# One block of a transformer with routed experts: the order of the opening's work is changed

## The chip, the cores and the metric

The kernel runs on one core of a Trainium2 chip. The metric is the device time of one execution in microseconds; before the change it is 890.94 us, the median of three runs (890.64 to 897.05).

## The reference

Input `x` is 32 batches of 256 tokens of 128 features. Each batch has its own modulation, made from a 32 x 128 condition `c`. An attention of 16 heads of 8 features stands ahead of a layer of 32 experts of which each token uses two. Cut to what matters:

```python
mod = (silu(c) @ wmod).reshape(32, 6, 1, -1)
sa, ca, ga, sb, cb, gb = (mod[:, i] for i in range(6))
ga = (2 * (ga >= 0) - 1) * maximum(abs(ga), 0.25)          # gb too
h = layernorm(x) * (1 + ca) + sa
Q, gate = split(h @ Wq + bq); K = h @ Wk + bk; V = h @ Wv + bv
Q, K = rmsnorm(Q, qn_w), rmsnorm(K, kn_w)                  # per head, 8 features
attn = softmax(Q @ K.T / sqrt(8))
x = x + ga * ((attn @ V * sigmoid(gate)) @ Wo + bo)
h = layernorm(x) * (1 + cb) + sb
vals, idx = top_k(softmax(h @ router_w.T), 2)
x = x + gb * sum_over_chosen(vals * (h @ expert_weights[idx]))
```

## The kernel before, in words

The kernel is written engine by engine. Each engine runs its own list of instructions in order and waits on semaphores; `sem` makes one, `then_inc` raises it, `wait` or `wait_ge` waits for it. Transfers raise a semaphore by 16 when they have landed.

After an opening, `run` goes through steps `s`. In a step each engine works on ten batches at different stages: `ahead` is batch s + 1, `b0` is batch s, `b1` the one before it, and so on. A batch goes through layer norm and projection (`b0`), splitting of q and k into bf16 parts which are stored to DRAM (`b1`) and loaded again as heads (`q_aug`, `k_aug`), row maxima of the scores (`b2`), exponentials and products with v (`b3`), output projection (`b4`), second norm and routing (`b5` to `b8`). Routed rows are scattered to DRAM (`xs_d`), and groups of them are multiplied by their expert's weights (`we`). The last steps drain this pipeline.

What the change touches is the opening and the first three steps:

- The condition. ScalarE takes an exponential into `sc` (L901), VectorE makes the silu from it by three operations (`sgn` L1181, `mag` L1183, `sc` L1185), TensorE transposes it and multiplies it by the first columns of `wmod` (L1706, L1710), ScalarE copies these as `saT` and `caT` (L956, L957).
- The bias. TensorE multiplies `saT` by the projection weights `wqkv` (L1714) once all eight pieces of weights and biases have landed (`w_ld`). VectorE adds the plain biases (`bias`, L1245), SyncE stores the sum to DRAM (L499) and loads it back, broadcast over partitions, as `bias_p` (L503). VectorE needs `bias_p` for `qkvg` (L1279), the projection's output. Ahead of the bias add, VectorE clears `zeros` (L1242).
- GpSimd scales the projection weights by `caT` (`scale_wqkv`, L679), and clears `k_aug`, `q_aug` (L659, L660) and `v_aug` (L684), of which it then sets one column of each head to one (L687).
- Five small late loads, issued by ScalarE (L961, L963): `rw` (router weights), `wo`, `bo_b` (output weights and bias), and the two norm weights into `w_col`. They share the semaphore `loads`. VectorE scales `w_col` (L1284) behind `qkvg`, and uses `bo_b` at the end of `mod_rows_out` (L1269), in step 1. TensorE transposes `rw` (L1758), ScalarE copies the result as `rwT` (L965).
- `squares` of batch 0 (L951) on ScalarE, whose sums VectorE takes (L1290) for the norms of q and k.
- In the step in which batch 0 is `b2`, `gate_exp` issues on ScalarE the store of the modulation `mod_d` (L976), the load of the expert weights `we` (L977, 2 MB in pieces of 512 bytes) and a store of zeros to the lead rows of four experts (`zero_leads`, L914, 256 KB). In the same step SyncE issues the four stores of batch 1's parts (`store_parts`, L530 and L533) and waits for them (`parts_st`) before it loads batch 1's heads (`load_heads`, L550, L554), on which TensorE's scores (L1779) wait.

Of the kernel before, what the change touches and what calls it, by code (L numbers as in the profile page):

```python
# [38 lines left out]
H, HD = 16, 8  # L39
# [142 lines left out]
def build(nc, x, Wq, bq, Wk, bk, Wv, bv, Wo, bo, qn_w, kn_w, router_w, expert_w, c_in, wmod, out):  # L182
# [10 lines left out]
    def sem(name):  # L193
        return ctx.enter_context(nc.semaphore(name))
# [4 lines left out]
    with ctx:  # L199
# [149 lines left out]
        loads, w_ld = sem("loads"), sem("w_ld")  # L349
        c_ld, wm_ld = sem("c_ld"), sem("wm_ld")  # L350
# [56 lines left out]
        def wait(eng, s, n):  # L407

            if isinstance(n, int) and n <= 0:
                return  # L410
            eng.wait_ge(s, n)
# [229 lines left out]
        def _(gp):  # L641
# [17 lines left out]
            nc.gpsimd.memset(k_aug[0][:].bitcast(F32), 0.0).then_inc(gp_const, 1)  # L659
            nc.gpsimd.memset(q_aug[0][:].bitcast(F32), 0.0).then_inc(gp_const, 1)  # L660
# [21 lines left out]
            scale_wqkv(Batch(0, 0, 0))  # L682
            for i in range(2):
                nc.gpsimd.memset(v_aug[i][:], 0.0).then_inc(gp_const, 1)  # L684
# [213 lines left out]
        def _(act):  # L898
# [60 lines left out]
            h1_transposed(Batch(0, 0, 0))  # L959
            for dst, src in ((rw[:], router_w), (wo[:], Wo), (bo_b[:], bo.partition_broadcast(NB))):  # L960
                act.dma_start(dst, src).then_inc(loads, 16)  # L961
            for k, w in enumerate((qn_w, kn_w)):
                act.dma_start(w_col[:, k:k + 1], w.unsqueeze(1).unsqueeze(2).broadcast_to([HD, H, 1])).then_inc(loads, 16)  # L963
            act.wait_ge(rwT_ps, 1)
            nc.scalar.activation(rwT[:], mx_ps[0][:].rearrange("p a b -> p (a b)")[:, 0:E], ACT.Copy).then_inc(rwT_done, 1)  # L965
            act.wait_ge(dve_const, 4)

            @of_batch
            def gate_exp(b):
# [4 lines left out]
                if b.n == 0:  # L974
                    act.wait_ge(mod_sb, 2)
                    act.dma_start(mod_d, mod[:]).then_inc(mod_st, 16)  # L976
                    act.dma_start(we[:].rearrange("k (e n) -> k e n", e=E), expert_w.rearrange("e k n -> k e n")).then_inc(we_ld, 16)  # L977
                if b.n < 8 * SETS:
                    zero_leads(b.n // 8, 4 * (b.n % 8), 4)

            @of_batch
            def high_part(b):

                wait(act, qkT_ps, b.n + 1)
# [102 lines left out]
            def attention_step(s, ahead, b0, b1, b2, b3, b4, b5, b6, b7, b8):  # L1087
# [35 lines left out]
                norms_seed(ahead, b0, b4)  # L1123
                router_exp(b7)
# [49 lines left out]
        def _(dve):  # L1174
# [72 lines left out]
            def mod_rows_out():  # L1247
# [20 lines left out]
                dve.wait_ge(loads, 16 * 5)  # L1268
# [14 lines left out]
            dve.wait_ge(loads, 16 * 5)  # L1283
# [418 lines left out]
        def _(pe):  # L1702
# [54 lines left out]
            pe.wait_ge(loads, 16 * 5)  # L1757
# [290 lines left out]
```

## Time and profile before

| | |
|---|---|
| median of three timed runs | 890.94 us (890.64 to 897.05) |
| the profiled execution | 899.71 us |
| its span, first to last instruction | 897.9 us |
| instructions | 23227 |
| mean granted clock of TensorE | 0.923 |

The span is what the rows below are measured in; the time of the same execution has 1.8 us around it. Times in the rows are microseconds from the start of the span. A row with an engine's name and a q (SPq, ACTq) is the issue of a transfer by that engine's queue, not the transfer; DMA rows tell of the transfers.

### The profile page before, as it was taken

The page shows a single profiled execution, that of the slowest core. Times are in us where ns is not written, and L with a number is a line of the kernel's source. Part 1 is how long each engine was busy: PE and PEld are TensorE (multiplying, and loading weights), DVE is VectorE, ACT ScalarE, POOL GpSimd, SP SyncE. Part 2 cuts the span into 40 slices and gives each one's busy share as a digit, 9 for nine tenths or more (in the row PEclk, how much of TensorE's full clock was granted, in tenths as well). Part 3 has the DMA queues.
Part 4 walks back from the last instruction along what each step waited for, and adds up shares of the span by engine and source line. Part 5 has one row for each costly group of instructions (what it writes and reads, how often), then busy time and mean ns, then how long its engine had stood idle before and what let it go on. Part 6 is the DMA issues. An engine that isn't in the chain of part 4 may idle for free. (4 is left out here: it accounts for less than half of the span.)

```text
span 897.9 us, 23227 instructions
## 1 busy us (share of the span) xinstructions
PE 697.3 (78%) x6142; PEld 467.0 (52%) x6142; DVE 666.9 (74%) x2007; ACT 576.5 (64%) x1313; POOL 528.4 (59%) x864
## 2 busy tenths in 40 slices
PE   3458898998899999898998798888988897564500
PEld 1225555655556666566665465556665556454400
DVE  5658888999998888887878877787877866643333
ACT  2227787888778887778887676677865775324400
POOL 4213346666566665555677666656666666575665
PEclk9559999999999999999999999999998999879955
DMA  2374556645656777666677666666666545789932
GB/s 72 78 187 107 149 134 155 165 129 160 143 154 170 183 186 182 168 170 176 178 199 210 169 167 173 159 167 167 175 160 160 156 143 168 205 232 271 287 97 78
DMA packets 189553, 147.98 MB, mean 165 GB/s; under 512 B 20596, under 2 KB 173908, under 8 KB 189428
## 3 DMA queue, kind: packets, MB, share of 16 engines
q1 hardware_dynamic: 122516, 99.41, 43.2%
q10 hardware_dynamic: 58720, 30.30, 11.9%
q0 software_dynamic: 8192, 16.79, 6.8%
q8 instruction: 56, 0.92, 0.5%
q14 instruction: 69, 0.57, 0.2%
HBM read 84.91 MB, written 60.95 MB: 162 GB/s over the span
## 5 line engine op out<-in xcount | busy, mean ns | idle before, releaser
L1310 DVE TENSOR_REDUCE negmax<-mx_ps 128x2 f32<-128x512 f32 x512 | 339.7, 685 | 64.2 <-PE mx_ps L1779 62.8
L1006 ACT ACTIVATE pr<-st_ps 128x512 f32<-128x512 f32 x512 | 289.8, 596 | 75.1 <-PE st_ps L1814 72.1
L1779 PE MATMUL mx_ps<-k_aug,q_aug 126*128 126x256 bf16 x1024 | 201.7, 282 | 66.2 <-DVE negmax L1310 36.9
L1814 PE MATMUL st_ps<-q_aug,k_aug 128*128 128x256 bf16 x1024 | 179.4, 277 | 11.7 <-ACT xsT L1042 8.4
L818 POOL DMA_INDIRECT xs_d<-h,slot x128 | 129.5, 1012 | 72.3 <-DVE slot L1413 48.9
L1779 PEld LDWEIGHTS mx_ps<-k_aug,q_aug 126*128 126x128 bf16 x1024 | 80.3, 99 | 160.5 <-issue 153.4
L833 POOL DMA_INDIRECT yg<-ys_d,gidx x128 | 124.8, 975 | 52.0 <-issue 36.7
L1828 PE MATMUL o_ps<-pr,v_aug 128*32 128x256 f32 x2048 | 137.0, 385 | 0.8 <-ACT oT L1012 0.2
L1814 PEld LDWEIGHTS st_ps<-q_aug,k_aug 128*128 128x128 bf16 x1024 | 98.6, 102 | 45.3 <-issue 30.2
L695 POOL TENSOR_TENSOR qn<-qkvg,rstd 128x256 f32<-128x256 f32 x64 | 39.2, 636 | 72.8 <-DVE rstd L1226 72.2
L1828 PEld LDWEIGHTS o_ps<-pr,v_aug 128*32 128x32 f32 x2048 | 54.8, 109 | 49.5 <-issue 28.4
L1492 DVE TENSOR_SCALAR yw<-yg,p_all 128x128 f32<-128x128 f32 x64 | 16.1, 297 | 69.0 <-DMA yg<-ys_d,gidx 44.8
L1042 ACT ACTIVATE xsT<-st_ps 128x512 f32<-128x512 f32 x72 | 42.6, 592 | 28.6 <-PE st_ps L1906 21.0
L1752 PE MATMUL misc<-wq_b,hT 128*128 128x400 f32 x128 | 58.1, 542 | 3.4 <-ACT hT L945 3.4
L1279 DVE TENSOR_TENSOR qkvg<-misc,bias_p 128x400 f32<-128x400 f32 x64 | 36.7, 575 | 28.8 <-PE misc L1752 22.3
L1012 ACT ACTIVATE oT<-o_ps 128x256 f32<-128x256 f32 x128 | 48.4, 378 | 9.6 <-PE o_ps L1828 9.5
L736 POOL TENSOR_TENSOR xga<-x_o,mod_o 128x256 f32<-128x256 f32 x31 | 22.5, 727 | 49.6 <-DMA mod_o<-mod_d 49.4
L1906 PE MATMUL st_ps<-ident,xs_sb 128*128 128x128 f32 x288 | 46.2, 285 | 6.1 <-DMA xs_sb<-xs_d 6.1
L1920 PE MATMUL st_ps<-we,xsT 128*128 x328 | 46.1, 284 | 5.9 <-issue 3.5
L708 POOL TENSOR_TENSOR parts<-rest,parts 128x512 bf16<-128x512 f32 x32 | 37.0, 1157 | 21.0 <-ACT parts L994 20.9
L1920 PEld LDWEIGHTS st_ps<-we,xsT 128*128 128x128 f32 x328 | 40.6, 194 | 12.2 <-issue 12.2
L1837 PE MATMUL misc<-ident,oT 128*128 128x128 f32 x256 | 41.3, 287 | 1.4 <-DVE table L1458 0.7
(169 smaller groups left out, 1192.5 us busy)
## 6 DMA issues: line engine op xcount, KB each, us to landing
ys_d<-ys_sb ACTq DMA_DIRECT2D x72, 256.0 KB
xs_sb<-xs_d SPq DMA_DIRECT2D x246, 64.0 KB
q_aug<-q_d SPq DMA_DIRECT2D x64, 192.0 KB
mod_o<-mod_d SPq DMA_DIRECT2D x32, 256.0 KB
bias_p<-bias_d SPq DMA_DIRECT2D x32, 200.0 KB, 4.6
q_d<-parts SPq DMA_DIRECT2D x32, 192.0 KB, 2.3
k_d<-parts SPq DMA_DIRECT2D x32, 192.0 KB, 2.5
k_aug<-k_d SPq DMA_DIRECT2D x64, 96.0 KB
```

The lines of the kernel that those rows point to most:

```text
L818: nc.gpsimd.indirect_dma_start(xs_d[chunk.set], bass.IndirectOffsetOnAxis(ap=slot[:, b.par, k:k + 1], axis=0), h2[:, b.par, k % TB, :], No ...
L833: nc.gpsimd.indirect_dma_start(yg[:, n % FB, k, :], None, ys_d[chunk.c], bass.IndirectOffsetOnAxis(ap=gidx[:, pair:pair + 1], axis=0)).the ...
L1006: nc.scalar.activation(pr[:, h % PR], st_ps[score_bank(b, h)][:], ACT.Exp, scale=SCALE).then_inc(exp_d, 1)
L1012: nc.scalar.activation(oT[:, g, :], o_ps[:, 0:NT], ACT.Copy).then_inc(oT_d, 1)
L1042: nc.scalar.activation(xsT[g % XB][:], in_bank(g), ACT.Copy).then_inc(xsT_d, 1)
L1310: v.tensor_reduce(negmax[:, :, h], mx_ps[h % 2][:], AX.X, ALU.max, negate=True).then_inc(mx_d, 1)
L1752: t_.matmul(bank[:, 0:QKVG], hT[:, t * P:(t + 1) * P], wq_b[:, b.par], start=True, stop=True).then_inc(qkv_ps, 1)
L1779: last = t_.matmul(mx_ps[h % 2][:, qc], q_aug[b.par][0:MROW, h, qc * P:(qc + 1) * P], k_aug[b.par][0:MROW, h, :], start=True, stop=True)
L1814: last = t_.matmul(st_ps[score_bank(b, h)][:, kc], k_aug[b.par][:, h, kc * P:(kc + 1) * P], q_aug[b.par][:, h, :], start=True, stop=True)
L1828: last = t_.matmul(o_ps[32 * j:32 * j + VW, 0:NT], v_aug[b.par][:, kc, h, :], pr[:, h % PR, kc, :], start=(kc == 0), stop=(kc == TB - 1))
L1906: last = t_.transpose(in_bank(g)[:, k * P:(k + 1) * P], xs_sb[:, g % XB, k, :], ident[:])
L1920: last = t_.matmul(out_bank(g)[:, k * P:(k + 1) * P], xsT[g % XB][:, k * P:(k + 1) * P], we[:, bass.ds(columns[k], P)], start=True, stop=True)
```

## The change

Three groups of work are put in another order; no operation is added or removed.

```diff
+        wc_ld = sem("wc_ld")
...
-            nc.gpsimd.memset(k_aug[0][:].bitcast(F32), 0.0).then_inc(gp_const, 1)
-            nc.gpsimd.memset(q_aug[0][:].bitcast(F32), 0.0).then_inc(gp_const, 1)
...
             scale_wqkv(Batch(0, 0, 0))
+            nc.gpsimd.memset(k_aug[0][:].bitcast(F32), 0.0).then_inc(gp_const, 1)
+            nc.gpsimd.memset(q_aug[0][:].bitcast(F32), 0.0).then_inc(gp_const, 1)
             for i in range(2):
                 nc.gpsimd.memset(v_aug[i][:], 0.0).then_inc(gp_const, 1)
...
+            for k, w in enumerate((qn_w, kn_w)):
+                act.dma_start(w_col[:, k:k + 1], w.unsqueeze(1).unsqueeze(2).broadcast_to([HD, H, 1])).then_inc(wc_ld, 16)
             for dst, src in ((rw[:], router_w), (wo[:], Wo), (bo_b[:], bo.partition_broadcast(NB))):
                 act.dma_start(dst, src).then_inc(loads, 16)
-            for k, w in enumerate((qn_w, kn_w)):
-                act.dma_start(w_col[:, k:k + 1], w.unsqueeze(1).unsqueeze(2).broadcast_to([HD, H, 1])).then_inc(loads, 16)
-            act.wait_ge(rwT_ps, 1)
-            nc.scalar.activation(rwT[:], mx_ps[0][:].rearrange("p a b -> p (a b)")[:, 0:E], ACT.Copy).then_inc(rwT_done, 1)
-            act.wait_ge(dve_const, 4)
...
                     act.dma_start(mod_d, mod[:]).then_inc(mod_st, 16)
-                    act.dma_start(we[:].rearrange("k (e n) -> k e n", e=E), expert_w.rearrange("e k n -> k e n")).then_inc(we_ld, 16)
                 if b.n < 8 * SETS:
                     zero_leads(b.n // 8, 4 * (b.n % 8), 4)
+                if b.n == 0:
+                    act.dma_start(we[:].rearrange("k (e n) -> k e n", e=E), expert_w.rearrange("e k n -> k e n")).then_inc(we_ld, 16)
...
             def high_part(b):
 
+                if b.n == 0:
+                    act.wait_ge(dve_const, 4)
...
                 norms_seed(ahead, b0, b4)
+                if s == 0:
+                    act.wait_ge(rwT_ps, 1)
+                    nc.scalar.activation(rwT[:], mx_ps[0][:].rearrange("p a b -> p (a b)")[:, 0:E], ACT.Copy).then_inc(rwT_done, 1)
...
-                dve.wait_ge(loads, 16 * 5)
+                dve.wait_ge(loads, 16 * 3)
                 v.tensor_tensor(mod[:, GABO * P:SB * P], mod[:, GA * P:GABO * P], bo_b[0:NB, :], ALU.mult).then_inc(mod_sb, 1)
...
-            dve.wait_ge(loads, 16 * 5)
+            dve.wait_ge(wc_ld, 32)
             v.tensor_scalar(w_col[:], w_col[:], W_SCALE, None, ALU.mult).then_inc(dve_const, 1)
...
-            pe.wait_ge(loads, 16 * 5)
+            pe.wait_ge(loads, 16 * 3)
             t_.transpose(mx_ps[0][:].rearrange("p a b -> p (a b)")[:, 0:E], rw[:], ident[0:E, 0:E]).then_inc(rwT_ps, 1)
```

What stands in a row on the engines is as follows. On GpSimd, in the opening, before:

```order
L657 IOTA past_pad 128x1
L659 MEMSET k_aug 128x2048
L660 MEMSET q_aug 128x2048
L679 TENSOR_TENSOR wq_b<-wqkv,caT 128x400
L684 MEMSET v_aug 128x1024 x2
L687 MEMSET v_aug 128x32 x2
L695 TENSOR_TENSOR qn<-qkvg,rstd 128x2x16x8 x2
```

And now on GpSimd, at the same place (line numbers are one or more off for the lines added and moved):

```order
L658 IOTA past_pad 128x1
L678 TENSOR_TENSOR wq_b<-wqkv,caT 128x400
L682 MEMSET k_aug 128x2048
L683 MEMSET q_aug 128x2048
L685 MEMSET v_aug 128x1024 x2
L688 MEMSET v_aug 128x32 x2
L696 TENSOR_TENSOR qn<-qkvg,rstd 128x2x16x8 x2
```

The two largest memsets have moved from ahead of the scaling to behind it. On ScalarE, from batch 0's transposed rows `hT` to the parts of its q and k, before:

```order
L945 ACTIVATE hT<-misc 128x256
L961 DMA rw<-in_L_ffn_router_w 32x128
L961 DMA wo<-in_L_attn_Wo 128x128
L961 DMA bo_b<-in_L_attn_bo 32x128
L963 DMA w_col<-in_L_attn_qn_w 128x1x1
L963 DMA w_col<-in_L_attn_kn_w 128x1x1
L965 ACTIVATE rwT<-mx_ps 128x32
L951 ACTIVATE sq<-qkvg 128x512
L928 ACTIVATE lnv<-mv,eps 128x66
L933 ACTIVATE y<-lnv 128x66
L987 ACTIVATE parts<-misc,w_col 128x256 x2
```

And now on ScalarE, at the same place:

```order
L946 ACTIVATE hT<-misc 128x256
L962 DMA w_col<-in_L_attn_qn_w 128x1x1
L962 DMA w_col<-in_L_attn_kn_w 128x1x1
L964 DMA rw<-in_L_ffn_router_w 32x128
L964 DMA wo<-in_L_attn_Wo 128x128
L964 DMA bo_b<-in_L_attn_bo 32x128
L952 ACTIVATE sq<-qkvg 128x512
L929 ACTIVATE lnv<-mv,eps 128x66
L934 ACTIVATE y<-lnv 128x66
L1127 ACTIVATE rwT<-mx_ps 128x32
L988 ACTIVATE parts<-misc,w_col 128x256 x2
```

The norm weights are now the first two of the five loads, and `rwT` has moved behind the norms' logarithm and exponential. On ScalarE, in the step in which batch 0 is `b2`, before:

```order
L973 ACTIVATE eg<-qkvg 128x32
L976 DMA mod_d<-mod 32x640
L977 DMA we<-in_L_ffn_expert_weights 128x32x128
L914 DMA xs_d<-zeros 128x4x128
L945 ACTIVATE hT<-misc 128x256
```

And now on ScalarE, at the same place:

```order
L971 ACTIVATE eg<-qkvg 128x32
L974 DMA mod_d<-mod 32x640
L915 DMA xs_d<-zeros 128x4x128
L978 DMA we<-in_L_ffn_expert_weights 128x32x128
L946 ACTIVATE hT<-misc 128x256
```

The expert weights and the zero leads have changed places.

## Rows read from the trace of the kernel before

**Rows 1.** The page, busy us (share of the span) of each engine

```profile
PE 697.3 (78%) x6142; PEld 467.0 (52%) x6142; DVE 666.9 (74%) x2007; ACT 576.5 (64%) x1313; POOL 528.4 (59%) x864
```

**Rows 2.** Window for L1006: us, ACT busy (count), PEclk, DMA share, GB/s

```profile
78.40:96.70 18.30, 8.79 (x16) 1.00 0.50 131
```

**Rows 3.** Timeline of VectorE: start, us, line, operation, [idle before <-releaser]

```profile
3.05 3.60 DVE L1181 TENSOR_SCALAR sgn<-sc 32x128 f32<-32x128 f32 x1
...
10.26 0.91 DVE L1242 MEMSET zeros<- 128x1024 f32 x1 [0.16 <-issue]
11.71 0.56 DVE L1245 TENSOR_TENSOR bias<-st_ps,bqkv 32x400 f32<-32x400 f32 x1 [0.54 <-PE st_ps L1714]
17.11 1.06 DVE L1279 TENSOR_TENSOR qkvg<-misc,bias_p 128x400 f32<-128x400 f32 x2 [4.83 <-DMA bias_p<-bias_d]
18.56 0.17 DVE L1284 TENSOR_SCALAR w_col<-w_col 128x2 f32<-128x2 f32 x1 [0.39 <-DMA w_col<-in_L_attn_kn_w]
...
19.61 0.69 DVE L1290 TENSOR_REDUCE mv<-sq 128x64 f32<-128x512 f32 x1
```

**Rows 4.** Instructions on tile sgn: duration ns min/median/max, first and last start

```profile
L1260 DVE TENSOR_SCALAR sgn<-mod x2: 208/211/214, 27.0 to 29.5; 32x128 f32<-32x128 f32 x2
```

**Rows 5.** Timeline of GpSimd

```profile
3.04 1.79 POOL L659 MEMSET k_aug<- 128x2048 f32 x1
...
4.78 1.79 POOL L660 MEMSET q_aug<- 128x2048 f32 x1
...
10.18 0.85 POOL L679 TENSOR_TENSOR wq_b<-wqkv,caT 128x400 f32<-128x400 f32 x1 [3.61 <-ACT caT L957]
...
10.97 1.84 POOL L684 MEMSET v_aug<- 128x1024 f32 x2
...
22.02 1.22 POOL L695 TENSOR_TENSOR qn<-qkvg,rstd 128x256 f32<-128x256 f32 x2 [8.94 <-DVE rstd L1226]
```

**Rows 6.** Timeline of TensorE, the bias matmul

```profile
10.09 1.51 PE L1714 MATMUL st_ps<-wqkv,saT 128*32 128x400 f32 x2 [0.38 <-ACT saT L956]
```

**Rows 7.** Timeline of ScalarE, opening

```profile
3.98 0.44 ACTq L906 DMA_DIRECT2D bqkv<-in_L_attn_bq  x1
...
14.94 0.62 ACTq L963 DMA_DIRECT2D w_col<-in_L_attn_kn_w  x1
...
18.95 0.62 ACT L951 ACTIVATE sq<-qkvg 128x512 f32<-128x512 f32 x1
```

**Rows 8.** Timeline of ScalarE, issues of expert weights and zero leads

```profile
45.06 0.83 ACTq L977 DMA_DIRECT2D we<-in_L_ffn_expert_weights  x1
...
45.92 5.68 ACTq L914 DMA_DIRECT2D xs_d<-zeros  x1
...
71.41 0.44 ACTq L914 DMA_DIRECT2D xs_d<-zeros  x1
```

**Rows 9.** Timeline of SyncE, stores of batch 1's parts

```profile
46.37 1.48 SPq L530 DMA_DIRECT2D q_d<-parts  x3
47.89 0.50 SPq L533 DMA_DIRECT2D k_d<-parts  x1
```

**Rows 10.** DMA, 46-51 us, then 51-57.2 us (q10 ScalarE's, q1 SyncE's): packets, MB

```profile
q10 hardware_dynamic: 553, 1.13, 86.3%
...
k_d<-parts SPq DMA_DIRECT2D x1, 192.0 KB, 9.2
...
q10 hardware_dynamic: 1015, 1.23, 60.1%
q1 hardware_dynamic: 1216, 0.59, 33.2%
```

**Rows 11.** Timeline of TensorE, scores of batch 1

```profile
61.77 1.01 PE L1779 MATMUL mx_ps<-k_aug,q_aug 126*128 126x256 bf16 x4 [6.17 <-DMA k_aug<-k_d]
```

**Rows 12.** DMA issues, 3 to 4.5 us: count, KB each, us to landing

```profile
bqkv<-in_L_attn_bq ACTq DMA_DIRECT2D x1, 2.0 KB, 3.3
```

**Rows 13.** DMA issues, 70 to 75 us, stores of batch 2's parts

```profile
k_d<-parts SPq DMA_DIRECT2D x1, 192.0 KB, 2.4
```

## The prediction

> **What bounds the kernel now.** I read the page first, for the shares: TensorE is busy 78% of the span, VectorE 74%, so no engine is saturated as a whole [rows 1]. Over most of the span the work is a pipeline of one batch per step; a step in it takes 18.3 us, in which ScalarE does the sixteen exponentials of a batch [rows 2]. None of its code changes, and nothing in it waits for a fixed moment. What the opening saves should therefore arrive at the end whole, and what it loses too. So I read the first 62 us engine by engine, and look for the last wait of each stage.
>
> Stage A is the conditioning path. VectorE's first real operation, `sgn`, starts at 3.05 us and takes 3.60 us [rows 3]. The same operation on the same tile shape takes 0.21 us later [rows 4]. In that stretch GpSimd runs two memsets of 1.79 us, until 6.57 us; `sgn` ends 0.08 us after the second [rows 3, 5]. The reader is to see an operation that is long only as long as GpSimd writes. From it hang `sc`, the transposes and matmuls on TensorE, `saT`, and with that the bias matmul at 10.09 us [rows 6].
>
> Stage B is the bias round trip: the add at 11.71 us, the store, the broadcast load; VectorE waits 4.83 us for it and starts `qkvg` at 17.11 us [rows 3]. The projection itself was ready earlier, so stage B decides.
>
> Stage C starts when `qkvg` ends at 18.17 us. VectorE waits 0.39 us more for the second norm weight, whose transfer was issued last of five, at 14.94 us; ScalarE does the squares at 18.95 us, behind `rwT`, for which it waits until all five transfers have landed [rows 3, 7].
>
> Stage D is the expert weights. ScalarE issues them at 45.06 us, and then stands 5.68 us in the issue of the zero leads, from 45.92 us on [rows 8]; `hT` and all else of it wait behind. SyncE issues the four stores of batch 1's parts from 46.37 us on; the last, `k_d`, at 47.89 us, lands 9.2 us later, at 57.09 us, and only then can the heads' loads be issued [rows 9, 10]. TensorE waits 6.17 us for these, until 61.77 us [rows 11]. Thus stage D's last wait is the transfer of the parts, not ScalarE.
>
> **The change, part by part.** *GpSimd's memsets behind the scaling.* `sgn` takes 0.21 instead of 3.60 us: minus 3.39 us at `sc`. The whole of it can't be kept, since the bias matmul also waits for all eight pieces of weights and biases. The last is issued by ScalarE at 3.98 us and lands 3.3 us later, at 7.28 us [rows 7, 12]. So the bias matmul starts at about 7.32 instead of 10.09 us: **minus 2.77 us**. Upstream work leaves room for that: shifted by 3.39 us it would stand at 6.70 us, or some tenths later, as batch 0's rows have to land as well. The add, the store, the broadcast load and `qkvg` follow unchanged, so `qkvg` starts at 14.34 us.
>
> The memsets themselves aren't gone: the scaling runs 7.3 to 8.2 us, then `k_aug` and `q_aug` (2 x 1.79 us) and `v_aug` (1.84 us) until some 13.7 us, the ones behind them to about 14 us. I cost them at nothing, as the bias round trip covers them: VectorE next has `qkvg` at 14.34 us, and GpSimd batch 0's normalised q and k, which stood at 22.02 us and move to 18.9 [rows 5]; SyncE's loads into `k_aug` and `q_aug` come later still. Without this cover they would cost up to 5.4 us. Inside the cover VectorE has two operations: the `zeros` memset and the bias add. Before, `zeros` took 0.91 us beside GpSimd's scaling and the add 0.56 us beside the `v_aug` memset, hardly more than `qkvg`'s 0.53 us each for as many columns [rows 3, 5]; I take both as undisturbed.
>
> *Norm weights first, `rwT` and a wait later.* The two norm weights are issued three transfers sooner and land before `qkvg` ends, so VectorE's 0.39 us go. The squares no longer stand behind `rwT`; then VectorE's order decides: `w_col`, statistics, aggregate, and the reduction at 19.61 us, all 0.38 us earlier with `w_col`. **Minus 0.38 us.** The three transfers behind them are issued later by the two issues of the norm weights. The router weights wait for the engine that does nothing before batch 0's q and k are there; the output bias is next read behind these; nobody waits. `rwT` now stands behind the norms' seed, where ScalarE waits for TensorE's transposes of them in any case. The wait on the scaled norm weights is long met where it now stands.
>
> *Zero leads ahead of the expert weights.* This frees ScalarE of most of 5.68 us: a later issue of zero leads takes 0.44 us [rows 8]. `hT` could come some microseconds sooner. But TensorE's next wait is on the parts, so **this part of it is worth nothing** on the path. It is `hT`'s followers on TensorE and VectorE that move into the idle time before 61.77 us. What is late next is `k_d`. In 46 to 51 us all packets are ScalarE's queue, 553 of them, none of SyncE's; in the 6 us after, SyncE's 1216 share with 1015 of ScalarE's [rows 10]. The parts are therefore served once the expert weights' descriptors are out. The new order changes this in two ways. The expert weights are asked for one issue later, 0.44 us, and with them the parts: plus 0.44. The 0.26 MB of zeros no longer move beside the parts; 51 to 57.2 us moved 1.23 + 0.59 MB, 0.29 MB per us [rows 10], so these are 0.9 us; most of it, I take 0.8: minus 0.8. Sum: **minus 0.36 us**, with bounds of plus 0.9 (the zeros' own bytes also push the expert weights back, and the parts gain nothing) and minus 0.9.
>
> One rule speaks on this place. The Trainium skill (DMA: Bandwidth & Descriptors, Queues, rings and completion order) says that each transfer engine takes turns between the queue rows that have work. By that rule the parts would move from 47 us on, with half of the rate, and the order of zeros and expert weights would be indifferent: minus 3.15 instead of minus 3.51. The trace disagrees here, with no packet of SyncE's queue before 51 us [rows 10], so I keep the sum from the rows.
>
> **Sum.** 2.77 + 0.38 + 0.36 = 3.51 us less. The profiled execution has a span of 897.9 us and a time of 899.71; so I expect a span of 894.4. The three timed runs have a median of 890.94, 8.8 us under the profiled time; the opening is the same work in both, and the difference is carried over: 890.94 - 3.5 = **887.4 us**.
>
> **The rivals.** *R1, the opening gives less (0 to 2 us).* Something other than the memsets holds `sgn`, or the weights land later than 7.28 us, or a few microseconds at the start are absorbed by waits further on. For it: only one row shows the long `sgn`. Against it: `sgn` ends with the memset to 0.1 us. Time: about 890.
>
> *R2, the memsets hold VectorE at a worse place.* If batch 0's statistics are late by about 0.8 us, the `zeros` memset reaches VectorE when GpSimd's row of memsets has begun. If it is held as `sgn` was, through one memset after the other, it starts at 13.7 and the bias add, queued behind it, at 14.6 us against 11.71: 2.9 us later than before. With the other parts kept (minus 0.74) that is plus 2.2: 893.1 us. It ends slower than before once the add starts later than 12.45 us. Against it: both operations ran undisturbed beside GpSimd's work, though `zeros` beside the scaling only.
> The Trainium skill (SBUF — State Buffer, SBUF: two separate sides) calls the shared ports an exclusive lock, held for a whole instruction by whoever starts first; that is what would do it. It agrees with the `sgn` row. A memset in place of `zeros` beside a memset is in no row here.
>
> *R3, the parts get ahead of the expert weights.* The expert weights' issue now ends at some 46.3 us in the old trace's times, and the first store of the parts is issued at 46.37. If the engines come to serve the stores first or in turns, `k_d` lands as batch 2's did, 2.4 us after its issue instead of 9.2 [rows 13]: up to 6.8 us, at least 2 to 5 of them real, since other waits (the maxima of batch 0, the norms) come next. Time: 882 to 886, say 884. Against it: three quarters of the stores are issued well behind.
>
> *R4, no change at all can be seen* because the steady part goes another way: timed runs of the same code stand at 890.64, 890.94 and 897.05. A median that falls on such an upper run would be near 893.
>
> **How the numbers follow.** My forecast (a gain of 2.0 to 4.7 us) 0.60; R1 0.17; R2 0.06; R3 0.10; R4 0.07. The likeliest case's own range is 886 to 889. For 8 in 10 the range takes in R1, most of R3 and the lower part of R2 and R4: 883.5 to 893. One per cent is 8.9 us, about what a measurement of this kernel can tell from no change; only R3 with everything on top reaches it (0.03), and only R4 with more bad luck on the other side (0.02). So 0.95 stays within 1%.
>
> **What would show it.** Right: `sgn` near 0.2 us with GpSimd idle beside it; the bias matmul at 7.2 to 7.5 us; `zeros` 0.9 and the bias add near 0.56 us; `qkvg` at 14.1 to 14.6; the squares directly behind it; the issue of the zero leads under 1 us; SyncE's first packets of the parts still some 5 us after their issue; TensorE's first scores of batch 1 at about 58.3 us; steps of 18.3 us thereafter. Wrong: `sgn` still long; the bias add after 12 us; `k_d` landing in under 4 us; or the step starts ahead by 3.5 us at 100 us and not at the end, which would mean the steady part absorbs a head start.

## The result and the profile after

The changed kernel takes 889.82 us, the median of 20 runs (885.75 to 897.29); the kernel before takes 893.96 us beside it, also 20 runs (889.85 to 898.71). The ratio is 0.9952, with a 95% interval of 0.9932 to 0.9973: 4.3 us less, between 2.4 and 6.1. That is less than 1%. The absolute time is 2.4 us above the forecast of 887.4, since the kernel before, measured more often, itself takes 3.0 us more than the 890.94 from which the forecast was counted. The profiled execution of the changed kernel took 894.12 us, with a span of 892.3 against 897.9 us. The busy times of the engines hardly move (TensorE 696.9 us against 697.3 [rows 1]), except VectorE's, which falls from 666.9 to 662.7 us: 3.45 of these 4.2 us are `sgn`, whose waiting the profile counts as busy time. No engine has less work to do; the gain is waiting time.

The timeline of VectorE in the changed kernel, the counterpart of [rows 3]. Columns as there: start, duration, engine, line, operation, and in brackets the idle time ahead of it and what ended it.

```profile
3.05 0.15 DVE L1185 TENSOR_SCALAR sgn<-sc 32x128 f32<-32x128 f32 x1
...
6.85 0.16 DVE L1236 SCALAR_TENSOR_TENSOR shift<-mv,rstd 128x2 f32<-128x2 f32 x1
7.17 0.91 DVE L1246 MEMSET zeros<- 128x1024 f32 x1 [0.16 <-issue]
8.60 0.56 DVE L1249 TENSOR_TENSOR bias<-st_ps,bqkv 32x400 f32<-32x400 f32 x1 [0.52 <-PE st_ps L1718]
...
14.50 1.06 DVE L1283 TENSOR_TENSOR qkvg<-misc,bias_p 128x400 f32<-128x400 f32 x2 [5.33 <-DMA bias_p<-bias_d]
...
15.47 0.16 DVE L1288 TENSOR_SCALAR w_col<-w_col 128x2 f32<-128x2 f32 x1
...
16.41 0.65 DVE L1294 TENSOR_REDUCE mv<-sq 128x64 f32<-128x512 f32 x1
```

`sgn` went from 3.60 to 0.15 us, and everything behind it is about 3 us earlier. One number stands against that: the wait of `qkvg` for the broadcast bias, 5.33 us, was 4.83.

GpSimd in the changed kernel, the counterpart of [rows 5]: the scaling first, the memsets behind it, and batch 0's normalised q and k.

```profile
7.08 0.85 POOL L678 TENSOR_TENSOR wq_b<-wqkv,caT 128x400 f32<-128x400 f32 x1 [3.98 <-DMA bqkv<-in_L_attn_bq]
...
7.87 1.80 POOL L682 MEMSET k_aug<- 128x2048 f32 x1
...
9.61 1.80 POOL L683 MEMSET q_aug<- 128x2048 f32 x1
...
11.36 1.85 POOL L685 MEMSET v_aug<- 128x1024 f32 x2
...
18.80 1.22 POOL L696 TENSOR_TENSOR qn<-qkvg,rstd 128x256 f32<-128x256 f32 x2 [5.32 <-DVE rstd L1230]
```

TensorE, the bias matmul and the first scores of batch 1 (before: [rows 6, 11]):

```profile
6.95 1.54 PE L1718 MATMUL st_ps<-wqkv,saT 128*32 128x400 f32 x2 [0.69 <-DMA bqkv<-in_L_attn_bq]
...
57.94 1.01 PE L1783 MATMUL mx_ps<-k_aug,q_aug 126*128 126x256 bf16 x4 [9.04 <-DMA k_aug<-k_d]
```

The scores start 3.83 us earlier, and TensorE waits for them longer than before, 9.04 against 6.17 us: what used to be spent behind ScalarE's stall is now spent waiting for the parts.

ScalarE around the expert weights (before: [rows 8]), and then SyncE's stores (before: [rows 9]):

```profile
41.60 0.45 ACTq L915 DMA_DIRECT2D xs_d<-zeros  x1
...
42.27 0.83 ACTq L978 DMA_DIRECT2D we<-in_L_ffn_expert_weights  x1
```

```profile
43.12 1.51 SPq L531 DMA_DIRECT2D q_d<-parts  x3
44.68 0.68 SPq L534 DMA_DIRECT2D k_d<-parts  x1
```

The DMA view of the changed kernel for 41 to 46 us and then 46 to 51 us (queue, packets, MB, share; for an issue its KB and us to landing), the counterpart of [rows 10]:

```profile
q10 hardware_dynamic: 768, 0.74, 59.2%
q1 hardware_dynamic: 1, 0.00, 0.0%
...
k_d<-parts SPq DMA_DIRECT2D x1, 192.0 KB, 8.6
...
q10 hardware_dynamic: 713, 1.46, 84.1%
q1 hardware_dynamic: 638, 0.32, 23.2%
```

ScalarE's 5.68 us in the issue of the zero leads are gone, and SyncE's queue still moves next to nothing (one packet) until about 46 us. `k_d` lands 8.6 us after its issue, at 53.28 us. At first it can't be the rate of transfer alone that the parts wait for: from 44 to 45 us, when the expert weights and the first stores of the parts have been asked for, 0.08 MB move, and from 48 to 49 us 0.36 MB. The stall was a symptom of the expert weights; the wait that decides is their other symptom, and it is still there.

### The profile page after: what moved, and what is told of

It reads as the page before. It is cut to its first block and busy times, and to the rows that moved or that the text cites. A ratio compares the mean times of both kernels' runs of the same rounds, so it can differ in the third digit from the quotient of the medians.

```text
span 892.3 us, 23227 instructions
## 1 busy us (share of the span) xinstructions
PE 696.9 (78%) x6142; PEld 467.6 (52%) x6142; DVE 662.7 (74%) x2007; ACT 576.9 (65%) x1313; POOL 530.2 (59%) x864
## 5 line engine op out<-in xcount | busy, mean ns | idle before, releaser
L819 POOL DMA_INDIRECT xs_d<-h,slot x128 | 129.9, 1015 | 70.9 <-DVE slot L1417 47.6
L1756 PE MATMUL misc<-wq_b,hT 128*128 128x400 f32 x128 | 57.2, 535 | 1.2 <-ACT hT L946 1.2
```

Source lines behind the costliest of these rows:

```text
L819: nc.gpsimd.indirect_dma_start(xs_d[chunk.set], bass.IndirectOffsetOnAxis(ap=slot[:, b.par, k:k + 1], axis=0), h2[:, b.par, k % TB, :], No ...
L1756: t_.matmul(bank[:, 0:QKVG], hT[:, t * P:(t + 1) * P], wq_b[:, b.par], start=True, stop=True).then_inc(qkv_ps, 1)
```

## The experiments

Medians and ratios come from several runs of each kernel against the kernel before on the same chip, except for e6, e7 and e8, of which there is one execution each. e5 to e8 were measured at another time than the rest, and beside them the kernel before takes 962.28 us instead of some 893, for a reason that the record doesn't show (it names the same chip for e1 to e4); their times are compared only with that, and their opening, which is the same there to 0.3 us, by the trace.

### e1: GpSimd's memsets alone

The kernel before, with this one edit:

```diff
-            nc.gpsimd.memset(k_aug[0][:].bitcast(F32), 0.0).then_inc(gp_const, 1)
-            nc.gpsimd.memset(q_aug[0][:].bitcast(F32), 0.0).then_inc(gp_const, 1)
     (scaling of the weights for batch 0)
+            nc.gpsimd.memset(k_aug[0][:].bitcast(F32), 0.0).then_inc(gp_const, 1)
+            nc.gpsimd.memset(q_aug[0][:].bitcast(F32), 0.0).then_inc(gp_const, 1)
```

> Only GpSimd's two memsets go behind the scaling; the five late loads, rwT, the expert weights and the zero leads stay as before. My theory: this is the larger part of the gain. sgn about 0.15 us, the bias matmul at about 6.95 us (3.1 us earlier), the four stores of batch 1's parts some 3 us earlier than before, but k_d still 9.2 us from issue to landing, scores of batch 1 at about 58.6 us, ScalarE's issue of the zero leads still near 5.7 us; in all 3 us less. On a question that the changed kernel leaves open: its bias round trip (add to qkvg) took 5.90 us instead of 5.40. If that comes of the norm weights' loads being issued first, here it is 5.40 again and qkvg starts at 14.0; if it comes of something else at the earlier moment, it is 5.9 here too. Rival (the memsets don't hold sgn): sgn stays near 3.6 us and nothing moves.

Measured: 889.44 us (12 runs) against 892.65 (35 runs), ratio 0.9953 (0.9926 to 0.9979). This is the ratio of the whole change. VectorE in e1:

```profile
8.72 0.56 DVE L1245 TENSOR_TENSOR bias<-st_ps,bqkv 32x400 f32<-32x400 f32 x1 [0.69 <-PE st_ps L1714]
...
14.12 1.06 DVE L1279 TENSOR_TENSOR qkvg<-misc,bias_p 128x400 f32<-128x400 f32 x2 [4.84 <-DMA bias_p<-bias_d]
```

From the add to `qkvg` e1 takes 5.40 us, just as before (11.71 to 17.11), and its `qkvg` is 0.38 us ahead of that of the full change. ScalarE's issue of the zero leads still takes 5.57 us, `k_d` lands 8.7 us after its issue, and yet the scores of batch 1 start at 57.74 us, not later than with the full change (58.6 had been expected). So the memsets' move carries all of the gain that can be measured.

### e2: the norm weights first, alone

The changed kernel, with GpSimd's memsets and the expert weights where they were before.

> Only the norm weights go first among the late loads, with a semaphore of their own, and rwT and the wait on the scaled weights go later; memsets, expert weights and zero leads as before. My theory: w_col without a wait behind qkvg, the reduction of batch 0's squares 0.4 us after where it would be counted from qkvg, so that GpSimd's first normalisation is 0.4 us nearer to qkvg (4.5 instead of 4.9 us). If the loads' order costs the bias round trip 0.5 us, qkvg itself is at 17.6 instead of 17.1 us and the sum is nothing; else the sum is minus 0.4 us. Either way the time can't be told from before's.

Measured: 893.41 us (12 runs), ratio 1.0005 (0.9974 to 1.0035). VectorE in e2:

```profile
11.72 0.56 DVE L1249 TENSOR_TENSOR bias<-st_ps,bqkv 32x400 f32<-32x400 f32 x1 [0.54 <-PE st_ps L1718]
...
17.62 1.06 DVE L1283 TENSOR_TENSOR qkvg<-misc,bias_p 128x400 f32<-128x400 f32 x2 [5.34 <-DMA bias_p<-bias_d]
...
18.59 0.16 DVE L1288 TENSOR_SCALAR w_col<-w_col 128x2 f32<-128x2 f32 x1
```

`w_col` no longer waits 0.39 us, as predicted. But `qkvg` starts at 17.62 instead of 17.11, 0.51 us later, with an unchanged add ahead of it. The wait was moved one operation forward, and `w_col` itself stands at 18.59 against 18.56. Batch 0's first `qn` on GpSimd comes at 21.92 against 22.02 us: from `qkvg` to `qn` it saves 0.61 us, the later `qkvg` costs 0.51, and 0.10 us is left.

### e7: the old order of the late loads in the changed kernel

```diff
-            for k, w in enumerate((qn_w, kn_w)):
-                act.dma_start(w_col[:, k:k + 1], ...).then_inc(wc_ld, 16)
     (router weights, output weights, output bias)
+            for k, w in enumerate((qn_w, kn_w)):
+                act.dma_start(w_col[:, k:k + 1], ...).then_inc(wc_ld, 16)
```

> The changed kernel, with the five late loads in the order of before (router weights, output weights and bias, then the norm weights), the norm weights keeping their own semaphore. If the norm weights' loads in front cost the bias round trip, as the two runs with and without them point to, qkvg starts 5.40 us after the bias add again, at 14.0 instead of 14.5 us; w_col then waits about 0.3 us for the second norm weight, the squares don't, and GpSimd's first normalisation comes at 18.6 instead of 18.8 us. If not, all of it stays.

VectorE in e7 (one execution), with GpSimd's scaling in a fence of its own:

```profile
7.10 0.82 DVE L1236 SCALAR_TENSOR_TENSOR shift<-mv,rstd 128x2 f32<-128x2 f32 x1
8.09 0.91 DVE L1246 MEMSET zeros<- 128x1024 f32 x1 [0.16 <-issue]
8.92 0.50 DVE L1249 TENSOR_TENSOR bias<-st_ps,bqkv 32x400 f32<-32x400 f32 x1
...
14.30 1.05 DVE L1283 TENSOR_TENSOR qkvg<-misc,bias_p 128x400 f32<-128x400 f32 x2 [4.88 <-DMA bias_p<-bias_d]
```

```profile
7.06 0.85 POOL L678 TENSOR_TENSOR wq_b<-wqkv,caT 128x400 f32<-128x400 f32 x1 [3.97 <-DMA bqkv<-in_L_attn_bq]
```

Undone, the round trip takes 5.38 us again, against 5.90 in the changed kernel; then `w_col` waits 0.42 us. From the add to `qn` it is 10.19 us, against 10.20: the two orders are worth the same. With e2 this shows both signs of the cost: it comes with the norm weights in front and goes with them behind. What costs is not shown. The store of the bias takes 1.6 us to land in e1 as in the changed kernel, so the 0.5 us lie in the broadcast load (3.4 against 3.8 us to land). The norm weights' own loads are issued beside it in the old order too (in e1 at 10.70 and 11.95 us, the broadcast load at 10.89), at no cost. What differs as much is the other three, 96 KB: they land 1.6 to 2.0 us after their issue in e7, ahead of most of the broadcast load, and 3.5 to 3.8 us in the changed kernel, beside it. No run separates these 96 KB from the order of the issues.

e7 also shows something nobody asked for. Batch 0's rows landed 0.25 us later here (its statistics start at 5.00 instead of 4.75 us), so `shift`, an operation on 128 x 2 elements, came 0.04 us after GpSimd's scaling had begun, and took 0.82 us instead of 0.16. It ends with the scaling. `zeros` stands behind it and the add behind that, at 8.92 instead of 8.60. The changed kernel's `shift`, at 6.85, clears the scaling at 7.08 by 0.07 us.

### e4: the memsets' cost doubled

The kernel before, with two more memsets of the same size on GpSimd behind those of `k_aug` and `q_aug` (the waits on their count two higher):

```diff
+            for half in range(2):
+                nc.gpsimd.memset(pr[:, 4 * half:4 * half + 4], 0.0).then_inc(gp_const, 1)
```

> The kernel before, with two more memsets of the same size (2 x 1.79 us, on a buffer not yet in use) behind k_aug's and q_aug's in front of the scaling. My theory, that VectorE's sgn is held until GpSimd's row of memsets is through, and that a shift in the opening arrives at the end: sgn takes about 7.2 us and ends at 10.3, the bias matmul starts at about 13.7, and the time is 3.6 us above before's. Rival A (sgn is long for a reason of its own): sgn 3.6 us as before, nothing else later than about 1 us. Rival B (the steady part absorbs shifts): the opening is 3.6 us late and the time is not.

Measured: 896.31 us (12 runs), ratio 1.005 (1.0021 to 1.0079), so 4.5 us more, between 1.9 and 7.1; the medians differ by 3.7. VectorE, GpSimd and TensorE in e4:

```profile
3.05 7.09 DVE L1183 TENSOR_SCALAR sgn<-sc 32x128 f32<-32x128 f32 x1
```

```profile
3.04 1.79 POOL L659 MEMSET k_aug<- 128x2048 f32 x1
...
6.53 3.54 POOL L662 MEMSET pr<- 128x2048 f32 x2
```

```profile
13.59 1.51 PE L1716 MATMUL st_ps<-wqkv,saT 128*32 128x400 f32 x2 [0.38 <-ACT saT L958]
```

`sgn` takes 7.09 us and ends at 10.14, 0.07 us after the fourth memset. It doesn't get in between any two of them. The bias matmul is 3.50 us later, and the time follows: a delay on this path arrives at the end, within the interval. That `sgn`'s length is GpSimd's memsets and nothing else is hereby shown from both sides. It isn't only memsets that do it: in the changed kernel the same operation on the modulation starts at 23.86 us, 0.02 us after a GpSimd tensor_tensor, and takes 1.21 us, until 0.08 us after that one's end. In the kernel before it starts as closely behind the same tensor_tensor (27.02 against 27.00 us) and takes 0.21.

### e8: what holds the bias matmul now

`wmod`, which SyncE loads ahead of the projection's weights, is loaded in two pieces, the second of them behind the weights.

```diff
-            sp.dma_start(wm[:], wmod).then_inc(wm_ld, 16)
+            sp.dma_start(wm[:, 0:2 * P], wmod[:, 0:2 * P]).then_inc(wm_ld, 16)
     (the projection's weights)
+            sp.dma_start(wm[:, 2 * P:], wmod[:, 2 * P:]).then_inc(wm2_ld, 16)
```

> The changed kernel, with the modulation weights loaded in two transfers, the two columns of blocks that the opening needs first (128 KB), the other four behind the rest of SyncE's loads. The claim of the prediction is that the bias matmul is capped by the last weight's landing, not by the conditioning path: with 256 KB less ahead of them the weights should land 0.5 to 0.7 us earlier, and the bias matmul start at 6.45 us, where saT (6.30 us) sets it. If the cap isn't the weights, it stays at 6.95.

The bias matmul in e8:

```profile
6.65 1.51 PE L1720 MATMUL st_ps<-wqkv,saT 128*32 128x400 f32 x2 [0.38 <-ACT saT L959]
```

With fewer bytes ahead of them the last piece lands 2.2 us after its issue instead of 2.9, and the matmul waits for `saT` again and not for a transfer. The cap that the prediction put on the gain is real, and in this one execution it goes with the bytes in front of the weights. The expectation had 6.45, but the matmul starts 0.34 us after `saT` (6.31), as it did before (9.75 and 10.09).

### e6: the `zeros` memset beside GpSimd's memsets

The rival R2 wanted `zeros` held by the row of memsets. Here it is put behind the bias add, where that row is surely running.

> The changed kernel, with VectorE's memset of zeros moved from ahead of the bias add to behind it. It starts then at about 9.2 us beside GpSimd's memsets of k_aug, q_aug and v_aug (7.9 to 13.2 us). My second rival of the prediction (a memset of VectorE is held by GpSimd's memsets as sgn was): zeros takes about 4 us, until 13.2 us. The other reading (a memset doesn't use what sgn had to wait for): 0.91 us as before. The bias add should start at 8.5 us in both, and qkvg at 14.5 us.

VectorE, then GpSimd, in e6:

```profile
9.51 0.91 DVE L1249 MEMSET zeros<- 128x1024 f32 x1 [0.16 <-issue]
```

```profile
8.06 1.81 POOL L682 MEMSET k_aug<- 128x2048 f32 x1
...
9.80 1.81 POOL L683 MEMSET q_aug<- 128x2048 f32 x1
```

The memset starts inside one of GpSimd's and ends inside the next, and takes its 0.91 us. R2's mechanism doesn't exist for this operation. A memset on VectorE isn't held; `sgn`, a tensor_scalar, and `shift`, a scalar_tensor_tensor, are.

### e3: the zero leads ahead of the expert weights, alone

The kernel before, with the issue of `we` moved behind the zero leads of batch 0.

> Only the expert weights go behind batch 0's zero leads. My theory: ScalarE's issue of the zero leads takes 0.45 instead of 5.7 us, hT of batch 2 comes 2.7 us sooner, and yet the scores of batch 1 start only 0.4 to 0.6 us earlier (61.2 us), since they wait for k_d, which lands about 8.6 us after its issue. In the time minus 0.5 us or nothing. Rival (ScalarE's stall was on the path): the scores and the time come 2.7 us or more earlier.

Measured: 893.65 us (12 runs), ratio 0.9993 (0.9964 to 1.0022). ScalarE and TensorE in e3:

```profile
44.60 0.45 ACTq L914 DMA_DIRECT2D xs_d<-zeros  x1
...
48.75 0.38 ACT L945 ACTIVATE hT<-misc 128x256 f32<-128x256 f32 x1 [3.17 <-PE misc L1743]
```

```profile
60.65 0.58 PE L1780 MATMUL mx_ps<-k_aug,q_aug 126*128 126x256 bf16 x2 [8.33 <-DMA k_aug<-k_d]
```

The stall is gone, `hT` is 2.95 us earlier (51.70 before), and nothing of it is seen in the time. The scores start 1.12 us earlier, of which 0.28 had come about before the swap (its first store is issued at 46.09, not 46.37). The steady number is the distance from that issue to the scores. In the kernels without the swap it is 15.40, 14.60, 15.32 and 15.22 us (before, e1, e2, e4), with it 14.82, 15.06, 14.56, 15.35, 14.64 and 15.26 (changed, its repetition e11, e3, e6, e7, e8). The means differ by 0.2 us and the runs by 0.8. Whether the swap gives anything on the path stays open.

It does change how the parts are served. From SyncE's first store's issue to its first packet it is 4.5 to 4.6 us in the four kernels without the swap, and 2.7 to 3.1 us in the six with it. But the parts that start sooner move beside more of the expert weights, at 128 packets per us (638 in 5 us, with 713 of ScalarE's) in the changed kernel, where they moved at 196 before (1216 in 6.2 us, with 1015 [rows 10]). `k_d` lands 8.7 to 9.2 us after its issue without the swap (before, e1, e2, e4) and 8.5 to 8.7 with it (changed, e3, e11).

### e5: the expert weights in eight pieces

If the parts wait for the expert weights' descriptors, smaller requests should let them through. The changed kernel, with four experts' weights asked for at each of the first eight batches:

```diff
-                if b.n == 0:
-                    act.dma_start(we[:]..., expert_w...).then_inc(we_ld, 16)
+                if b.n < 8:
+                    act.dma_start(we[:, 4*b.n*P:4*(b.n+1)*P]..., expert_w[4*b.n:4*(b.n+1)]...).then_inc(we_ld, 16)
...
-                        pe.wait_ge(we_ld, 16)
+                        pe.wait_ge(we_ld, 16 * 8)
```

> The changed kernel, with the expert weights loaded in eight pieces of four experts, one in each step from batch 0's on, each behind the zero leads of that step; they are needed first in step 14. My theory: the parts of batch 1 wait for the descriptors of 2 MB of expert weights; with a piece of 256 KB k_d lands 3 to 4 us after its issue instead of 8.6, and the scores of batch 1 start 4 to 5 us earlier (53 to 54 instead of 57.9 us). Later steps stay at 18.4 us, since a piece beside zeros and parts is 0.9 us of transfer beside work. In all 4 us less than the changed kernel, 8 less than before (ratio 0.991). Rival (something else of that stage comes next, such as batch 0's maxima or TensorE's slow clock): scores at 56 us or later, time 1 to 2 us less than the changed kernel.

Measured: 960.99 us (12 runs) against 962.28, ratio 0.9977 (0.9937 to 1.0017). No gain was shown, where the theory had some 0.9% to give. TensorE at the scores of batches 1 and 3, and the windows of the two steps behind (us, busy time and count of TensorE, its weight loads, VectorE, ScalarE, GpSimd; granted clock, DMA share, GB/s):

```profile
51.85 0.91 PE L1784 MATMUL mx_ps<-k_aug,q_aug 126*128 126x256 bf16 x4 [2.30 <-DMA k_aug<-k_d]
...
90.73 1.01 PE L1784 MATMUL mx_ps<-k_aug,q_aug 126*128 126x256 bf16 x4 [3.12 <-DMA k_aug<-k_d]
```

```profile
68.61:88.68 20.07, 16.20 (x154) 10.06 (x154) 15.98 (x39) 14.13 (x32) 5.33 (x10) 1.00 0.54 134
88.68:111.57 22.89, 18.68 (x154) 11.41 (x154) 16.11 (x39) 14.79 (x35) 6.78 (x12) 0.85 0.53 128
```

At batch 1 there is more than the 4 to 5 us expected: the scores start 6.4 us before those of e6 (58.27), a changed kernel measured at the same time. The two steps of the windows, which start 6.5 us and 5.2 us before e6's, end 1.1 us before (111.57 against 112.70), and by 153.53 us e5 is 1.3 us behind. Two things take the lead. Each piece now travels beside a batch's own parts: from 60 to 215 us, in eight waits, TensorE stands 17.6 us before the heads' loads have landed, against 10.3 in e6. And the granted clock of the second step is 0.85, where TensorE is busy 18.68 us instead of the 16.26 that the same step takes at 1.00 in e9 below; e5 has thirteen steps at a reduced clock, e6, e7 and e8 have eight or nine. Whether the pieces bring these about no run shows, so only the waits are the pieces' known price. A head start is worth something only if it isn't paid for in the later steps.

### e9 and e10: the expert weights in the opening

Between 18 and 25 us nothing moves in the kernel before. The 2 MB fit there whole: ScalarE asks for them behind batch 0's squares.

```diff
-                if b.n == 0:
-                    act.dma_start(we[:]..., expert_w...).then_inc(we_ld, 16)
     (in the step that holds batch 0's squares, behind these)
+                if s == 0:
+                    act.dma_start(we[:]..., expert_w...).then_inc(we_ld, 16)
```

> The changed kernel, with the whole of the expert weights asked for in the opening, behind batch 0's squares on ScalarE (at about 15.6 us), where before and after the change no transfer runs from 18 to 25 us. Splitting them over eight steps gave the scores of batch 1 six microseconds and took them back in the next steps. My theory: what costs is expert weights beside the stores of parts, in whichever step; here they are beside none. The stores of batch 1's parts then land 3 us after their issue, its scores start at 51.5 to 52 instead of 57.9 us, and the later steps keep their 18.4 us, so that the time is 5 to 6 us less than the changed kernel's, 9 to 10 less than before (ratio 0.990). Risk: 2 MB take 7 us, until 24 us, and the first stores of parts come at 25 us. Rival (a head start gained in stage D is always taken back by the next steps): the time is the changed kernel's within 2 us although the scores start 6 us sooner.

The window of 18 to 25 us, in the kernel before and then in e9 (columns as above: the last two are DMA share and GB/s):

```profile
18.00:25.00 7.00, 1.36 (x5) 0.85 (x5) 2.60 (x11) 1.88 (x6) 2.96 (x3) 0.58 0.00 0
```

```profile
18.00:25.00 7.00, 1.44 (x6) 1.01 (x6) 3.45 (x11) 2.29 (x6) 3.95 (x4) 0.50 1.00 289
```

DMA issues in e9, SyncE's store and TensorE's scores of batch 1, and the two steps that e5 had lost in:

```profile
we<-in_L_ffn_expert_weights ACTq DMA_DIRECT2D x1, 0.5 KB, 10.1
...
k_d<-parts SPq DMA_DIRECT2D x1, 192.0 KB, 2.1
```

```profile
44.48 0.45 SPq L534 DMA_DIRECT2D k_d<-parts  x1
...
51.15 0.60 PE L1783 MATMUL mx_ps<-k_aug,q_aug 126*128 126x256 bf16 x4 [1.42 <-DMA k_aug<-k_d]
```

```profile
68.56:87.39 18.83, 16.20 (x154) 10.05 (x154) 15.98 (x39) 14.03 (x32) 5.35 (x10) 1.00 0.50 133
87.39:105.95 18.56, 16.26 (x154) 10.10 (x154) 15.98 (x39) 14.68 (x35) 6.75 (x12) 1.00 0.56 136
```

Measured: 882.63 us (6 runs) against 893.21 (17 runs), ratio 0.9883 (0.9847 to 0.9919), 10.4 us less than before. `k_d` lands 2.1 us after its issue instead of 8.6 with almost the same issue time, the scores stand at 51.15, and the steps behind are undisturbed. From the first store's issue to SyncE's first packet it is 0.9 us now. This shows by taking the cause away that stage D's wait was the expert weights' load.

e10 adds e8's split and has SyncE issue the norm weights.

> The same, and besides the modulation weights in two transfers and the norm weights loaded by SyncE in the opening's first loads instead of by ScalarE. Theory: bias matmul at 6.6 us, qkvg at 13.5 to 13.7 us (its round trip 5.4 us, without the norm weights' loads beside it), GpSimd's first normalisation at 17.9 instead of 18.8 us, the rest as in the kernel above: 1 us less than that. Risk: GpSimd's scaling starts before VectorE's shift and holds it for 0.7 us.

Measured: 883.75 us (6 runs), ratio 0.9903 (0.9865 to 0.994). Its opening is the earliest of all (bias matmul 6.65, add 8.27, `qkvg` 13.77, `qn` 18.06 against 18.96 in e9), and its scores of batch 1 come at 50.84 against 51.15 us: of 0.9 us two thirds go before they reach the first scores. Between e9 and e10 the measurement can't tell.

### e11: the changed kernel again

> The changed kernel once more, on the same chip as the two others. Theory: ratio to before 0.995, sgn 0.15 us, qkvg about 14.5 us. The opening's margins can be read again: whether shift is held by the scaling as in the run with the old load order (there shift took 0.82 us, since batch 0's rows landed 0.25 us later).

Measured on e9's chip: 890.12 us (10 runs), ratio 0.9964 (0.9938 to 0.999). Its scores of batch 1 start at 58.17 us, after a wait of 8.51 us (9.04 in the first trace of this kernel). The ratio puts the changed kernel 0.9 to 5.5 us below the kernel before here, so its gain is less sure than the first interval alone says. e9 beats both kernels of this case, the changed one by some 7 us; that is near the 6.8 us by which `k_d` of batch 1 lagged behind that of batch 2 before [rows 10, 13].

## Why the prediction was right, and where it wasn't

The forecast was 3.5 us less and the result is 4.3 (2.4 to 6.1); direction, size and the term that carries it were right. The absolute 887.4 was 2.4 us too low: the result, 889.82, lies in the stated 883.5 to 893, but outside the likeliest case's own 886 to 889, because the 890.94 it was counted from was a median of three. The sum holds up because one term carries it; the smaller terms were off, and that their errors cancel is luck.

**Stage A, 2.77 us: right, a little small.** The mechanism is shown by e1 and e4, and its cap by e8. The bias matmul moved from 10.09 to 6.95 us, 3.14 us. The cap was read from a landing 3.3 us after the issue [rows 12]; it took 2.9 here. The add moved 3.11 us.

**Stage B, "follow unchanged": this step failed.** The prediction moved the norm weights' loads three issues forward and asked who waits for the others. It didn't ask what then runs beside the broadcast load of the bias. Add to `qkvg` went from 5.40 to 5.90 us. The seven kernels with the norm weights' loads in front have 5.75 to 6.06 (the changed one and e2 5.90, e11 5.88, e9 5.89, e6 and e8 5.75, e5 6.06); the five with the old order have 5.38 to 5.52 (before and e1 5.40, e7 5.38, e4 5.47, e3 5.52). e10, where SyncE loads the norm weights before the add, has 5.50, and its three other loads land 1.8 to 1.9 us after their issue, as in the old order. So the cost of the order is shown, and its cause, as said under e7, stays open.

**Stage C, 0.38 us: the mechanism right, the worth wrong.** VectorE's wait is gone and the squares follow `qkvg` directly (15.59 against 18.95 us). From `qkvg` to `qn` it gave 0.61 us, but stage B takes most of that back, so the part is worth 0.10 us at `qn` (e2), and nothing that can be seen in the time. Stages A to C together gave 3.22 us at the first `qn` (22.02 to 18.80), against the 3.15 forecast: 0.34 more in A, 0.50 less in B and 0.23 more in C, which cancel.

**Stage D, 0.36 us: right that ScalarE's stall was off the path; the two terms behind the 0.36 were not what happens.** e3 takes away 5.2 us of stall for nothing. The prediction had the parts start later with the expert weights, plus 0.44 us, and expected "still some 5 us" from their issue to their first packets. They start sooner instead: 2.8 us after the first store's issue, against 4.6 before. And the 0.8 us of zeros no longer beside them aren't gained as such, since more of the expert weights moves beside them. What is left at `k_d` is 0.6 us from issue to landing (9.2 to 8.6), less than the scatter of the scores behind it, 0.8, so that the 0.36 is neither confirmed nor refuted. The rule of turns between queue rows that have work (the Trainium skill, DMA: Bandwidth & Descriptors, Queues, rings and completion order) agrees with the trace from the first packet of the parts on: 638 packets of SyncE's to 713 of ScalarE's in 5 us. It doesn't account for the 2.8 us before it; that the parts wait there for the expert weights' descriptors is the likely reading, but no trace shows descriptors. e9 shows what having the queues to themselves gives the parts: 2.1 us from issue to landing.

**The later steps: "arrive at the end whole" is true on average only.** After 57.94 us the head start shrinks from 3.8 to 3.1 us over the next step, and two more pieces go in single steps. Windows of such steps of the changed kernel, with the same two of the kernel before under them in a fence of their own:

```profile
94.72:115.08 20.36, 16.26 (x154) 10.11 (x154) 15.98 (x39) 14.68 (x34) 6.81 (x12) 1.00 0.53 134
...
189.19:209.52 20.33, 18.61 (x166) 11.92 (x166) 17.40 (x52) 15.28 (x37) 12.49 (x24) 0.92 0.51 139
```

```profile
98.09:116.72 18.63, 16.26 (x154) 10.10 (x154) 15.99 (x39) 14.67 (x34) 6.74 (x12) 1.00 0.58 136
...
191.12:210.03 18.91, 17.10 (x166) 11.02 (x166) 17.23 (x52) 15.26 (x37) 12.43 (x24) 1.00 0.57 149
```

In the first pair the busy times and clocks are equal, and 1.7 us are a wait: TensorE waited 3.2 us for the heads' loads where it had waited 1.4 before, 1.5 in e1 and 1.8 in e11. In the second, TensorE's granted clock is 0.92 instead of 1.00, its busy time 1.5 us longer and the step 1.4 us. The kernel before has such dips at other places, five of them between 512 and 637 us against four, so that a head start of 0.5 us at 210 us is 3.8 at 706 and 5.6 at the end. The profiled executions of e1 to e4, e9 to e11 and this pair have six to eight of these steps each. They are the likeliest source of R4, the spread of some 12 us between runs of one kernel: of the 35 runs of the kernel before beside e1, the three fastest (887.07 to 888.03 us) have mean granted clocks of 0.930 to 0.933 and the three slowest (898.04 to 899.47) 0.913 to 0.921. But no run takes the steps away to show it.

**The rivals.** R1 (0 to 2 us) fell with `sgn`, and is outside the measured interval, though not outside that of e11 (0.9 to 5.5). R2 fell by its mechanism: the operation it named isn't held (e6). It had also left out half of the rule that it cites: the Trainium skill (SBUF — State Buffer, SBUF: two separate sides) limits the lock, on VectorE's side, to operations in a mode that uses two ports, and to those with two inputs in SBUF against a GpSimd operation that reads SBUF. With that limit the traces agree as far as they go: `shift` has two inputs, the scaling reads, and it is held in e7; `zeros` reads nothing and isn't held in e6; `sgn` has one input and is held through four memsets in e4, which by that rule needs the mode with two ports, and no row shows the mode. R2 had the right danger at the wrong operation: `shift` clears the scaling by 0.07 us, and missing it costs 0.3 us (e7), not 2.9. R3 didn't happen, though its price was real: e9 got 7 us by having the parts alone in the queues, where the forecast gave 2 to 5 of 6.8. R4's scatter showed in the starting point: the median of three before the change stood 3.0 us below that of twenty.

## What to carry to other kernels

When an operation is many times longer than its twin, look at what the other engines write in just that stretch, and put their bulk work where the waiting engine has nothing to do; here that was all of the gain. When transfers change places, cost what runs beside the new place as well as who waits at the old one, and when a stall is removed, follow the wait that ends last, since the stall and that wait can be two symptoms of one large load. The cure for such a load is a stretch where the queues are empty, not smaller pieces beside the work.

## What the runs showed of the hardware

- One load of 2 MB in rows of 512 bytes, asked for by ScalarE, and followed by a store of 256 KB of zeros, kept SyncE's later stores from moving a packet for 4.5 to 4.6 us after their issue (before, e1, e2, e4), and blocked ScalarE's own next issue for 5.68 us. With the zeros ahead of it, it was 2.7 to 3.1 us (changed, e3, e6, e7, e8, e11), and with no such load 0.9 us (e9, e10). In the opening the load took 10.1 us to land (e9); the window of 18 to 25 us moved 289 GB/s with a DMA share of 1.00.
- GpSimd's memsets of 128 x 2048 elements hold a 32 x 128 tensor_scalar of VectorE through as many of them as follow each other (3.60 us for two, 7.09 for four). They don't hold a memset of VectorE, 0.91 us beside them (e6) as without. GpSimd's tensor_tensor holds a 128 x 2 scalar_tensor_tensor (0.82 against 0.16 us, e7), and the tensor_scalar too (1.21 against 0.21 us, changed kernel at 23.86 us).
- Two loads of single elements issued ahead of three loads of 96 KB in all, instead of behind them, lengthened a store and broadcast load issued beside them from 5.38 to 5.52 us to 5.75 to 6.06 (five and seven kernels).
- The kernel before takes 893 us beside e1 to e4 and e9 to e11, and 962 beside e5 to e8, with a mean granted clock of about 0.90 instead of 0.92. The changed kernel's opening events are equal to 0.3 us in both. Why is not shown.
